# The order in which a fused gated cross-attention kernel loads x, K and V, changed for one core of Trainium2

## The reference

```python
def _L0_xattn_ref(memory, query, b, seq_len):        # 16 heads of 8 features
    k_mem, v_mem = jnp.split(memory, 2, axis=2)
    Q = _split_heads(query, NUM_HEADS) * dh ** (-0.5)
    logits = jnp.einsum('bhqd,bhkd->bhqk', Q, Kh) + b
    logits = logits + MASK_VALUE * (1.0 - valid)[:, None, None, :]
    weights = jax.nn.softmax(logits, axis=-1)
    out = jnp.einsum('bhqk,bhkd->bhqd', weights, Vh)
...
x = x + jnp.tanh(g_xattn[0]) * _L0_xattn_ref(ctx_2048, _layernorm(x), L0_xattn_b, itok)
x = x + jnp.tanh(g_ffn[0]) * _L0_ffn_ref(_layernorm(x), ...)     # top-2 of 8 experts, 512 hidden units
```

## Time and profile before

| | |
|---|---|
| time, median of 3 runs | 273.34 us (271.56 to 273.58) |
| the profiled execution's own time | 274.92 us |
| its span, first to last instruction | 273.1 us |
| PE, DVE, POOL, ACT busy | 241.7, 214.5, 165.8, 160.6 us |
| mean granted TensorE clock | 0.975 of full speed |

### The profile page before, as it was taken

One profiled execution on the slowest core, in us unless ns is written; L12 is line 12 of the kernel. 1 busy time (PEld: TensorE's weight loads), 2 busy tenths in 40 slices (PEclk: granted clock), 3 DMA queues, 4 the chain that ended last, 5 costly groups with the idle time before them and its releaser, 6 DMA issues.

```text
span 273.1 us, 8107 instructions
## 1 busy us (share of the span) xinstructions
PE 241.7 (89%) x3000; PEld 184.4 (68%) x3000; DVE 214.5 (79%) x621; ACT 160.6 (59%) x316; POOL 165.8 (61%) x311
## 2 busy tenths in 40 slices
PE   1477678979899899989999999999999999999995
PEld 0365445556566566656666689798888889897865
DVE  6888976989999899998949788978785858585442
ACT  8649776878888788986778642423333342424230
POOL 7899893867868586776885739392909150505110
PEclk9997759999999999999999999999999999999999
DMA  3999998695989766560000000101010101000011
GB/s 91 246 175 174 214 220 145 171 210 121 237 166 228 134 161 135 140 114 10 8 4 4 2 0 1 42 0 38 2 38 0 42 0 41 0 21 18 11 29 38
DMA packets 49472, 23.46 MB, mean 86 GB/s; under 512 B 7667, under 2 KB 49307, under 8 KB 49435
## 3 DMA queue, kind: packets, MB, share of 16 engines
q1 hardware_dynamic: 48931, 22.83, 40.6%
q10 hardware_dynamic: 504, 0.12, 0.3%
HBM read 7.29 MB, written 2.10 MB: 34 GB/s over the span
## 4 chain that ended last, share of the span: by engine, by line
PE 65%; DVE 12%; POOL 7%; issue 6%; DMA 4%; ACT 4%; SPq 1%; ACTq 0%; POOLq 0%
PE bank L1141 25%; PE bank_max L1176 10%; DVE negmax L1367 8%; PE bank L1083 7%; PE bank L1051 6%; PE bank L1118 3%; PE bank L1094 3%; PE bank L1134 2%; DMA stack<-max_rows 2%; PE bank L1057 2%; DMA stack<-part 2%; DVE rest L1313 2%; ACT probs L829 2%; PE bank L1107 1%; PE bank_max L1012 1%
## 5 line engine op out<-in xcount | busy, mean ns | idle before, releaser
L1367 DVE TENSOR_REDUCE negmax<-bank 128x4 f32<-128x512 f32 x128 | 82.8, 679 | 11.4 <-PE bank L1051 9.5
L829 ACT ACTIVATE probs<-bank 128x512 f32<-128x512 f32 x128 | 72.1, 602 | 18.5 <-PE bank L1057 17.2
L1141 PE MATMUL bank<-u_part,b_part 128*128 128x512 f32 x192 | 51.9, 399 | 0.1
L1051 PE MATMUL bank<-stack 64*128 64x128 bf16 x432 | 40.3, 222 | 11.5 <-issue 3.8
L869 ACT ACTIVATE h<-bank,bi_col 128x512 f32<-128x512 f32 x32 | 22.0, 687 | 47.5 <-PE bank L1141 47.5
L1057 PE MATMUL bank<-stack 64*128 64x128 bf16 x512 | 47.9, 222 | 0.3
L1051 PEld LDWEIGHTS bank<-stack 64*128 64x128 bf16 x432 | 25.1, 96 | 27.3 <-DVE negmax L1367 17.1
L1083 PE MATMUL bank<-probs,vpad 128*32 128x128 f32 x1024 | 41.7, 281 | 0.0
L1141 PEld LDWEIGHTS bank<-u_part,b_part 128*128 128x128 f32 x192 | 35.5, 189 | 8.2 <-ACT h L869 0.5
L665 POOL TENSOR_TENSOR x_part<-KV,x_part 128x512 fp32r<-128x512 f32 x8 | 10.4, 1299 | 49.9 <-ACT x_part L851 49.9
L1490 DVE SCALAR_TENSOR_TENSOR hsum<-bank,nbi_col,h 128x512 f32<-128x512 f32 x32 | 24.0, 749 | 20.9 <-PE bank L1141 20.8
(11 more groups left out here) (142 smaller groups left out, 423.9 us busy)
## 6 DMA issues: line engine op xcount, KB each, us to landing
stack<-part SPq DMA_DIRECT2D x96, 128.0 KB, 4.7
KV<-in_ctx_dram SPq DMA_DIRECT2D x9, 256.0 KB, 5.7
X<-in_x_dram SPq DMA_DIRECT2D x7, 256.0 KB, 6.4
out_dram<-res SPq DMA_DIRECT2D x7, 256.0 KB, 2.3
KV<-in_ctx_dram SPq DMA_DIRECT2D x3, 512.0 KB, 7.3
stack<-bias_line SPq DMA_DIRECT2D x7, 48.0 KB
stack<-max_rows SPq DMA_DIRECT2D x13, 24.0 KB
X<-in_x_dram SPq DMA_DIRECT2D x2, 128.0 KB, 2.8
```

The lines of the kernel that those rows point to most:

```text
L829: act.activation(probs[:, i % 4, :], sc2[i % 2][:, :], ACT.Exp).then_inc(s_exp, 1)
L1051: mm = pe.matmul(first_bank(m, c)[:, j * 128:(j + 1) * 128], stack[at, s, h0 + 2 * j, q0:q0 + 128], stack[at, s, h0 + 2 * j, 512 + q0:640 ...
L1141: mm = pe.matmul(dst, w[a], v[b], start=(start and k == 0), stop=(closed or (stop and k == 2)), skip_group_check=closed)
L1367: dve.tensor_reduce(negmax[:, p % 2, n % 2, 8 * (u // 2) + u % 2:8 * (u // 2) + u % 2 + 7:2], bank_cols(first_bank(n, c)), AX.X, ALU.max, ...
```

## The change

Only SP's and DVE's programs change; no instruction is added or dropped. On SP, k3 moves from before pair 0's transfers to before pair 1's, x4 from there to round 0, and v0 from before pair 1 to the end of round 0. In the main loop, x5 goes from round 0 to 1, v1 from the end of round 1 to that of round 2, and k5 and x6 from round 2 to 3; then v2 to v4 move from the ends of rounds 3, 5, 7 to those of 4, 6, 8, and kv6 with x7, kv7 with x8, and kv8 from the heads of rounds 4, 6, 8 to those of 5, 7, 9. On DVE a fill of slot 1 moves behind the variances of batch 2, and the statistics of samples 8 to 11 move behind `first_rest(1)`, a fill of slot 2 and `third_part(1)`.

```diff
@@ -463,13 +463,11 @@
             load_x(3)
-            load_k(3)
-            load_x(4)
             pair_to_stack(0, 0)
             pair_to_stack(0, 1)
             pair_to_stack(0, 2)
             bias_to_stack(sp, 0)
-            load_v(0, 4)
+            load_k(3)
             pair_to_stack(1, 0)
@@ -478,11 +476,13 @@
             for q in range(PAIRS + 1):
-                if q in (0, 2):
-                    load_k(q // 2 + 4)
-                elif q // 2 + 4 < len(BATCHES) and q % 2 == 0:
+                if q in (0, 3):
+                    load_k(q // 3 + 4)
+                elif q % 2 == 1 and 5 <= q and q // 2 + 4 < len(BATCHES):
                     load_kv(q // 2 + 4)
-                if q // 2 + 5 < len(BATCHES) and q % 2 == 0:
+                if q == 0:
+                    load_x(4)
+                elif q % 2 == 1 and q // 2 + 5 < len(BATCHES):
                     load_x(q // 2 + 5)
@@ -497,8 +497,8 @@
-                if q in (1, 3, 5, 7):
-                    load_v(2 * q + 2, 2 * q + 6)
+                if q % 2 == 0 and q <= 8:
+                    load_v(2 * q, 2 * q + 4)
@@ -1334,7 +1334,6 @@
             dve.tensor_copy(slot_words(0, 2), word_of(2)).then_inc(s_ones[0], 1)
-            dve.tensor_copy(slot_words(1, 1), word_of(1)).then_inc(s_ones[1], 1)
             first_rest(0)
@@ -1348,15 +1347,16 @@
             variances(2)
+            dve.tensor_copy(slot_words(1, 1), word_of(1)).then_inc(s_ones[1], 1)
             dve.tensor_copy(slot_words(1, 3), word_of(3)).then_inc(s_ones[1], 1)
+            first_rest(1)
+            dve.tensor_copy(slot_words(2, 2), word_of(2)).then_inc(s_ones[2], 1)
+            third_part(1)
             for n in range(8, 12):
                 stats_of(n)
             for n in range(8, 12):
                 aggregate(n)
             variances(3)
-            first_rest(1)
-            dve.tensor_copy(slot_words(2, 2), word_of(2)).then_inc(s_ones[2], 1)
-            third_part(1)
```

## The result

| | before | after |
|---|---|---|
| time, median | 273.26 us (270.83 to 277.14, 20 runs) | 275.76 us (272.33 to 278.99, 20 runs) |
| the profiled execution's own time | 274.92 us | 273.49 us |
| its span | 273.1 us | 271.7 us |

The ratio of the times is 1.0078, with a 95% interval of 1.0046 to 1.0110: the change makes the kernel 0.8% slower.

A forecast was written before the change was run, and what follows sets the result against it. DMA engines are 90% busy or more in most slices to 100 us; between transfer waits DVE bounds the loop, PE close behind. 0 + 1.2 - 1.2 - 1.3 + 1.1 = -0.2 us gave 273.1 us, range 270.2 to 276.9.

The forecast's parts named there:

- slower rival: Late loads decide: x4 +2.1, V +3.7, only the 1.2 us at 44.01 gained; +4.6, 277.9 us, chance 0.24.
- the rule: Skill's advice to issue transfers early and wait late; by it only the x4 and V terms count, +2.3 us.
- the two lateness terms: Waits for loads issued later: DVE's for x4, +1.2 us, and POOL's for V, +1.1 us.
- DVE move: Start: statistics moved to DVE's idle time, first row maximum some 0.5 us later; cost 0, from -0.4 to +0.5 us.
- x4: Near 29.5 us DVE waits 2.0 us for this load, partly covered before sample 5; +1.2 us (0 to +2.1).
- pair 1's maxima: Fewer loads ahead of this transfer in round 2, so sample 7's stop goes; -1.2 us (0 to -1.2).
- stops of samples 15 and 19: Loads no longer ahead of pairs 5 and 7's max_rows, so stops of 0.42 and 0.86 us go; -1.3 us.
- V: POOL waits in rounds 3, 5, 7, 9 before copies to vpad, v3 felt by TensorE; +1.1 us, at worst +3.7.
- the 1.19 us of 44.01: "Issue" time on the chain ahead of sample 7's scores, read as pair 1's max_rows landing late.
- cover of 0.73 us ahead of sample 5: DVE's idle time at 35.80 for pair 0's max_rows, expected to absorb part of x4's wait.
- The even pairs: Their max_rows now have loads ahead but should hold: cost 0, up to +1.2; stops at 13, 17, 21 would refute.
- the 1.36 us at 59.72: Stop between sample 11's first and second step, no transfer awaited; cause unnamed, gone only in the faster rival, chance 0.18.

The follow-up runs named there:

- e5: The changed kernel with v1 to v4 back in their old rounds; 274.46 us, ratio 1.0093 to the kernel before.
- e7: The changed kernel with x4 back ahead of pair 0 and v1 to v4 back in their old rounds; 271.98 us, ratio 1.0005 to before.
- e8: The changed kernel once more, unaltered, for a second trace; 275.08 us, ratio 1.0093 to the kernel before.
- e6: The changed kernel with x4 back ahead of pair 0's transfers; 274.13 us, ratio 1.0032 to the kernel before.
- e15: The kernel before with only x5 moved to round 1 and k5, x6 to round 3; 272.40 us, ratio 1.0001.
- e16: The kernel before with only kv6 with x7, kv7 with x8, and kv8 moved to rounds 5, 7, 9; 272.04 us, ratio 1.0003.
- e2: The kernel before with only k3 moved to just before pair 1, x4 into round 0, v0 to its end; 273.20 us, ratio 1.0057.
- e4: The kernel before with only DVE's order at the start changed as in the change; 271.88 us, ratio 1.0035.
- e11: The kernel before with max_rows issued ahead of the kv and x loads in rounds 4, 6, 8; 271.60 us, ratio 0.9973.
- e13: The kernel before with only x4 moved to round 0 behind k4; 273.09 us, ratio 1.0036.
- e3: The kernel before with only k5, x5 to x8 and kv6 to kv8 a round later; 272.87 us, ratio 1.0028.
- e12: The kernel before with DVE part, k3, v0, x5, k5, x6 as changed, and max_rows ahead of loads in rounds 4, 6, 8; 271.65 us, ratio 0.9995.
- e14: The changed kernel with x4 issued between the transfers of pairs 1 and 2; 273.10 us, ratio 1.0023 to the kernel before.
- e1_v_only: The kernel before with only v1 to v4 a round later; 275.60 us, ratio 1.0111.
- e10: The changed kernel with max_rows issued at the head of rounds 5, 7, 9, ahead of the loads; 275.45 us, ratio 1.0140 to before.

## Why the prediction was wrong

The forecast was 273.1 us and no change. The time, 275.8 us, is within its range, but the direction is the slower rival's, and its loss is half of that rival's. That rival's worst case is also said to be the rule's; by the rule, which counts the two lateness terms alone, the worst would be 2.1 + 3.7 = 5.8 us, not 4.6. The terms as measured:

| term | forecast us | measured |
|---|---|---|
| DVE move | 0 (-0.4 to +0.5) | alone +0.35% (+0.06 to +0.64), 0.9 us |
| x4 | +1.2 | alone +0.36%, 1.0 us; within the change 0.9%, 2.4 us (e5 against e7), or 0.6%, 1.6 us (e8 against e6) |
| pair 1's maxima | -1.2 | 0 (e15: -0.3 to +0.3%) |
| stops of samples 15 and 19 | -1.3 | 0 (e16: -0.4 to +0.4%) |
| V | +1.1 | alone +1.1%, 3.0 us; within the change 0 to 0.3% (e8 against e5, e6 against e7) |

**The step that failed** is "I take the 1.19 us of 44.01 as gone: -1.2", and with it "Their stops of 0.42 and 0.86 us go: -1.3". That they would be gone from the trace was right; that the time would go with them was not. Two things were wrong in it. The 1.19 us was only partly a loss: of what sample 7 gives back, sample 8 takes 0.8 us, since within sample 7 TensorE then waits for ACT (the 0.77 us above). And I counted three stops of one execution as if each stood in all of them. That execution was itself 1.7 us longer than the median of the 20 runs. TensorE stops ahead of sample 7 in only two other traces (e2 1.26, e4 0.73 us). In e11 and e13 it doesn't stop there and sample 7 has its 1.2 us of extra time all the same; TensorE's granted clock from 41 to 44 us was 0.66 and 0.50 in them, and 1.00 in e15. The stops of 15 and 19 are each 1.3 us or less where they occur, and they move about: the kernel before with only the DVE part changed has 0.5 us at 15 and nothing at 19, with only x4 moved 1.3 us at 15 and nothing at 19. Without the two gains my own sum gives 273.1 + 2.5 = 275.6 us. It is the figure that the paragraph on the rule led to (+2.3 us, the two lateness terms alone). That it is so near the measured time is partly luck, since x4 cost more than its 1.2 us and V less than its 1.1. For x4 and V early loads were right before, as the Trainium skill has it (DMA: Bandwidth & Descriptors, Rules for kernel authors), and the runs agree, with nothing lost once both are early again (e7, 1.0005). The other loads could go out later at no net cost.

**x4** came close to the forecast, but for its cover: issued at 25.25 (forecast 25.5 to 26.6), in use 5.5 us later (5.7), DVE idle 2.04 us (2.0). The cover of 0.73 us ahead of sample 5 was again of that one execution: e15, e16 and e11, in which nothing of the start is moved, start sample 5 at 34.94, 34.00 and 34.34, before's trace at 35.80, and in none of the three is TensorE's last wait ahead of it one for `max_rows`. So x4's delay was not covered: sample 5 starts 2.1 us later in after than in e7, and within the change x4 cost up to twice the 1.2.

**V** came in mechanism, in the four rounds named, but not in place. I had v3 as the one that TensorE feels, at 4.8 us; it took 3.2 and v4 took 4.8 (91.14 - 86.31), with 1.01 us on TensorE. The size was too large for the whole change, where x4's wait seems to cover it, and too small for the part alone, where kv and x stand ahead of V.

**The even pairs** were the failure that I named and priced at nothing ("since 1 MB directly ahead cost 5.4 us, it should hold"). It doesn't, and stops ahead of 13, 17 and 21 were the sign that I had named for being wrong. The stop ahead of 21 is 1.40 us of TensorE's idle time in e3, 1.04 in e5 and 2.09 in e7, e16 has 0.97 ahead of 17, and the change itself, in e8, 2.98 ahead of 13 and 2.01 ahead of 17. The clearing, the bias and the transfer between did not save it: from issue to use `max_rows` took 3.8 us (e7), 4.8 (e16), 5.8 and 6.3 (e8) and 7.4 (e6). In the first trace of after sample 21's 0.7 us is the wait behind v4. That the stop is the landing of `max_rows` rests on whose scores stop, on where the stops stand in all the traces, and on their absence where the maxima go first; no trace names the releaser.

**The DVE move** gave a first maximum at 18.65 and not 19.0 (in e4, alone, at 19.08). Alone it costs a little; in e7 and e12, which contain it, nothing is seen of it. What it delays stays open, and so does the 1.36 us at 59.72. It is of another kind than the stops above: it stands within the matmuls of one step, where the program waits for no semaphore. None of the 17 other traces has it in that place; two have the like ahead of sample 20, e15 with 0.61 us and e11:

```profile
90.41 0.21 PE L1053 MATMUL bank<-stack 64*128 64x128 bf16 x1 [1.07 <-issue]
```

## What to carry over

A load may move later only as far as its landing, at the slow end of what such loads take (here 5.7 us for 256 KB, where other loads of that size were in use after 2.8 to 4.8), still comes ahead of its reader; e14 gave 5.9 us back to one load, and what is left of the loss can't be told from nothing. A stop counts as a gain only if it stands in several executions, and only less what the next wait in line takes over, so price what one trace shows as a gain with care, and a new wait in full. Moving large loads from ahead of one small urgent transfer to ahead of the next moves the stop with them. Putting the small transfer ahead of early loads (e11) is worth trying, but its gain here was barely clear of nothing.

## What the runs showed that I had not expected

In `e1_v_only` the wait of 3.06 us on TensorE was followed by half clock. The windows from 78 to 90 us (length; busy time and count of PE, PEld, DVE, ACT, POOL; then the granted clock, the DMA share and GB/s):

```profile
78.00:81.00 3.00, 0.04 (x1) 0.04 (x2) 1.00 (x3) 1.05 (x3) 2.46 (x8) 0.81 0.52 128
81.00:84.00 3.00, 3.00 (x40) 1.88 (x42) 1.29 (x2) 0.86 (x2) 2.84 (x8) 0.50 0.76 197
84.00:87.00 3.00, 3.00 (x48) 2.00 (x48) 2.40 (x5) 2.51 (x6) 1.38 (x4) 0.55 0.42 126
87.00:90.00 3.00, 3.00 (x70) 2.07 (x68) 2.68 (x7) 2.23 (x5) 2.78 (x10) 1.00 0.58 142
```

TensorE was granted 0.50 and 0.55 for the next six microseconds, its lower level of 1.2 GHz, and issued 40 and 48 matmuls in windows in which it later issued 70. Sample 17 took 4.0 us of extra time for a wait of 3.06. The 2.09 us in e7 were followed by three windows of 3 us (from 94 us) at 0.62, 0.81 and 1.00, and the 3.65 us in e6 by 0.50, 0.50 and 0.99 (from 69 us), with 4.0 and 1.6 us of extra time at samples 13 and 14. So a wait of this kind can cost more than its length.

The length of the one wait doesn't decide it, though. The clock fell behind 1.40 us in e3 (0.79 and 0.64 from 95 us) and stayed at 1.00 behind 1.36 in before (59.72), 1.01 in after and 1.92 in e10 (ahead of 81.08).

The start stands partly at the lower level in every kernel. The page's rows of the granted clock, before and after, in slices of 6.8 us:

```profile
PEclk9997759999999999999999999999999999999999
PEclk9997858999999999999999999999999999999999
```

In after the clock was 0.50 from 35 to 41 us and 0.77 from 41 to 44; in e7 it was back at 1.00 from 41 us on. How long the stretch lasts is not a matter of x4 alone: in e11, with x4 early, it was 0.66 from 41 to 44.
